# Opening of a fused four-layer kernel: loads on two queues, semaphores per use, second x slice early, first query rows copied from two queues

## The reference, cut to what matters

```python
x = x + attn(layernorm(x), Wq, Wk, Wv, Wo, Wg1, Wg2, norm_w)     # 16 batches x 256 x 128
x = x + moe(layernorm(x), router, w1, w3, w2, ws1, ws3, ws2)
x = x + conv_scan(layernorm(x), w_in, conv_w, conv_b, w_B, w_C, w_out)
x = x + fp4_ffn(layernorm(x), w_gate, w_up, w_down)
```

```python
q = silu(xn @ Wq);  k_raw = xn @ Wk;  v = xn @ Wv
z = cumlogsumexp([0, k_raw]);  k = exp(k_raw - z[1:]);  g = z[:-1] - z[1:]
q, k = rope(q), rope(k)                       # each twice as wide, cos and sin
o = causal_linear_attention(q, k, v, decay=g)
o = o * sigmoid(xn @ Wg1 @ Wg2)
x = x + (o * rsqrt(mean(o*o) + 1e-6) * norm_w) @ Wo
```

## Time and profile before

| | us |
|---|---|
| median of 3 runs | 609.23 (608.47 to 613.55) |
| the profiled execution, its time | 605.77 |
| the profiled execution, its span | 604.0 |
| PE busy | 542.9 (90% of the span) |
| DVE busy | 447.0 (74%) |
| POOL busy | 339.1 (56%) |
| ACT busy | 316.2 (52%) |
| mean granted TensorE clock | 0.973 |

### The profile page before, as it was taken

How to read it: one execution, slowest core, us unless ns; L and a number is a source line. 1 busy time by engine, 2 the same in 40 slices (tenths; PEclk the granted TensorE clock), 3 DMA queues, 4 the chain that set the end, 5 groups by cost and what they waited for, 6 DMA issues and landing times. The chain is left out here.

```text
span 604.0 us, 15157 instructions
## 1 busy us (share of the span) xinstructions
PE 542.9 (90%) x4517; PEld 444.8 (74%) x4518; DVE 447.0 (74%) x1179; ACT 316.2 (52%) x899; POOL 339.1 (56%) x514
## 2 busy tenths in 40 slices
PE   1799999999999898988999997998999999999966
PEld 1567667766777577788998986787788777887754
DVE  2689999899888549943457543478999999998873
ACT  2355766666666554415565652345545564556432
POOL 5468777777776622247567105556666775763231
PEclk9999999999999999998999998998999999999975
DMA  7000100110010155012522211100111111110000
GB/s 210 24 20 29 46 28 27 43 35 26 35 43 27 56 167 139 1 27 61 146 69 56 40 36 30 18 10 9 24 31 18 17 22 30 17 17 9 10 19 17
DMA packets 35193, 25.55 MB, mean 42 GB/s; under 512 B 4752, under 2 KB 31568, under 8 KB 35152
## 3 DMA queue, kind: packets, MB, share of 16 engines
q1 hardware_dynamic: 29264, 20.32, 11.5%
q0 software_dynamic: 5888, 4.72, 5.1%
HBM read 14.09 MB, written 6.75 MB: 34 GB/s over the span
## 5 line engine op out<-in xcount | busy, mean ns | idle before, releaser
L1149 PE MATMUL a_ps_a<-a_qx,a_kt 32*128 32x512 f32 x512 | 69.1, 628 | 1.0 <-DMA a_qx<-a_qs 1.0
L1712 POOL DMA_INDIRECT x<-yg_dram,pos x32 | 55.9, 1747 | 11.6 <-issue 11.6
L1316 POOL TENSOR_TENSOR d_hq<-d_fh_v,d_fh_scale 128x352 f32<-128x352 f32 x32 | 27.9, 888 | 61.3 <-DVE d_fh_v L1342 61.3
L442 POOL TENSOR_SCALAR_AFFINE_SELECT a_at<-a_at 128x512 f32<-128x512 f32 x80 | 50.5, 650 | 14.6 <-ACT a_at L523 14.6
L199 POOL DMA_INDIRECT rows<-xn_dram,slot_token x40 | 40.1, 1003 | 25.3 <-ACT c_rows L1478 11.0
L523 ACT ACTIVATE a_at<-a_ps_a 128x512 f32<-128x512 f32 x80 | 44.5, 600 | 11.6 <-PE a_ps_a L1149 10.0
L1521 DVE TENSOR_TENSOR c_hid<-c_act,c_ps 128x352 f32<-128x352 f32 x39 | 20.2, 518 | 36.4 <-ACT c_act L1464 36.4
L1149 PEld LDWEIGHTS a_ps_a<-a_qx,a_kt 32*128 32x128 f32 x512 | 31.7, 188 | 16.9 <-issue 16.3
L207 PE MATMUL d_ps_A<-d_xnT,wmix 128*128 128x256 f32 x128 | 37.1, 290 | 0.6 <-ACT d_silu L1794 0.6
L715 DVE TENSOR_TENSOR a_at<-a_ps_a,mask 128x512 f32<-128x512 f32 x48 | 32.8, 684 | 6.4 <-PE a_ps_a L1149 5.2
L208 PE MATMUL d_ps_A<-d_xnT,wmix 128*128 128x256 f32 x128 | 36.1, 282 | 0.0
(11 more groups left out here) (347 smaller groups left out, 1758.3 us busy)
## 6 DMA issues: line engine op xcount, KB each, us to landing
a_qx<-a_qs SPq DMA_DIRECT2D x64, 64.0 KB, 1.9
a_at<-in_L_ffn_w_eDF_dram SPq DMA_DIRECT2D x16, 176.0 KB, 3.2
yg_dram<-c_y SPq DMA_DIRECT2D x19, 128.0 KB, 1.8
xn_dram<-a_xn2s SPq DMA_DIRECT2D x16, 128.0 KB, 1.9
out_dram<-x SPq DMA_DIRECT2D x16, 128.0 KB, 1.9
w<-in_L_ffn_w_eFD_dram SPq DMA_DIRECT2D x2, 512.0 KB, 5.7
x<-in_L_attn_x_dram SPq DMA_DIRECT2D x1, 768.0 KB, 5.4
rows<-xn_dram,slot_token POOLq DMA_INDIRECT x40, 2.8
```

The source lines that it names most:

```text
L442: nc.gpsimd.affine_select(at[:, t, r, :, :], at[:, t, r, :, :], pattern=[[0, 4], [1, P]], compare_op=ALU.is_ge, fill=0.0, base=0, channel_ ...
L1149: last = nc.tensor.matmul(ps_a[:, r, :, :], kt[rows, b.par, c_, tile(t)], qx[rows, b.par, :, c_, tile(t)], start=(c_ == 0), stop=(c_ == 1))
L1712: nc.gpsimd.indirect_dma_start(out=x[:, t, :], out_offset=None, in_=g["yg_dram"][:, :], in_offset=bass.IndirectOffsetOnAxis(ap=g["pos"][:, ...
```

## The change

The loads are dealt out anew. ACT's queue takes the mask, Wg1 and Wg2, counted on a semaphore of their own, `s_wg`, for which alone PE's first transpose waits. SP's queue keeps x's first four tiles, Wk, Wq and Wv (`s_wq`, now three transfers); behind them come tiles 4 to 7 of x (`s_x2nd`, batches 2 and 3), the rope tables, the block mask, then Wo, norm_w and the router, which now count on `s_ws` with the two shared-expert weights. The rest of x comes in pieces of 12 tiles.

DVE begins with batch 0's statistics, behind the wait for x alone. `weights()` follows, in the same iteration: it rearranges Wk and Wq and makes the halves of 384 columns, then waits for ACT's product of Wg1 and Wg2 and makes those of the last 128. `weights_late()` scales Wo an iteration later, after batch 0's low half, behind a wait for the five transfers of `s_ws`. POOL zeroes `a_qx` after batch 0's `norm_sums` and no longer at the start. Of the first batch's four query transfers, SP issues two and ACT two, which ACT does after the steps of iteration -2, behind a wait for the scaled queries. PE waits for `s_prep_dve` at counts 5 and 6 before the gate product and the product with Wo of batch 0.

```diff
@@ SP
-            sp.dma_start(wg1[:, :], io["L0_attn_Wg1"]).then_inc(s_wq, 16)
-            sp.dma_start(wg2[:, :], io["L0_attn_Wg2"]).then_inc(s_wq, 16)
-            sp.dma_start(mask[:, :, :], io["c_mask"].rearrange("p (a b) -> p a b", a=3)).then_inc(g["s_const"], 16)
+            sp.dma_start(x[:, 4:8, :], xr[:, 4:8, :]).then_inc(s_x2nd, 16)
             sp.dma_start(rope[:, :, :], io["c_rope"].rearrange("p (a b) -> p a b", a=2)).then_inc(g["s_const"], 16)
             sp.dma_start(block[:, :], io["c_block"]).then_inc(g["s_const"], 16)
-            sp.dma_start(wo[:, :], io["L0_attn_Wo"]).then_inc(s_wq, 16)
-            sp.dma_start(normw[:, :], io["L0_attn_norm_w"].rearrange("(p a) -> p a", a=1)).then_inc(s_wq, 16)
-            sp.dma_start(router[:, :], io["L0_ffn_router_DE"]).then_inc(s_wq, 16)
+            sp.dma_start(wo[:, :], io["L0_attn_Wo"]).then_inc(s_ws, 16)
+            sp.dma_start(normw[:, :], io["L0_attn_norm_w"].rearrange("(p a) -> p a", a=1)).then_inc(s_ws, 16)
+            sp.dma_start(router[:, :], io["L0_ffn_router_DE"]).then_inc(s_ws, 16)
...
-            for a, b_ in ((4, 16), (16, 32)):
+            for a, b_ in ((8, 20), (20, 32)):
                 sp.dma_start(x[:, a:b_, :], xr[:, a:b_, :]).then_inc(g["s_x1"], 16)
...
-                    for h in range(4):
+                    for h in range(2 if j.m is None and j.off == 0 else 4):
@@ POOL
-            nc.gpsimd.memset(qx[:, :, :, :, :], 0.0).then_inc(s_zero, 1)
...
-                    pool.wait_ge(g["s_const"], 48)
+                    pool.wait_ge(g["s_const"], 32)
...
                 norm_sums(j + 3, mv[:, :, :], rstd[:, :], shift[:, :], s_ln1, s_xn, s_nb1)
+                if j.m is None and j.off == -3:
+                    nc.gpsimd.memset(qx[:, :, :, :, :], 0.0).then_inc(s_zero, 1)
@@ ACT
+            act.dma_start(mask[:, :, :], io["c_mask"].rearrange("p (a b) -> p a b", a=3)).then_inc(s_wg, 16)
+            act.dma_start(wg1[:, :], io["L0_attn_Wg1"]).then_inc(s_wg, 16)
+            act.dma_start(wg2[:, :], io["L0_attn_Wg2"]).then_inc(s_wg, 16)
             act.wait_ge(s_prep, 1)
...
+                if j.m is None and j.off == -2:
+                    act.wait_ge(s_zero, 2)
+                    act.wait_ge(s_qs, 1)
+                    for h in range(2, 4):
+                        act.dma_start(qx[h::4, 0, h, :, :].rearrange("p c n -> p (c n)"),
+                                      qs[h::4, 0, :, :].rearrange("p c n -> p (c n)")).then_inc(s_qx[0], 16)
@@ DVE
-            dve.wait_ge(s_wq, 16 * 8)
-            for n in range(2):
-                nc.vector.tensor_copy(wall[:, P * n:P * n + P].rearrange("p (r i s) -> p r s i", r=4, s=4),
-                                      wload[:, n, :].rearrange("p (r s i) -> p r s i", r=4, s=4))
-            nc.vector.tensor_scalar(wo[:, :], wo[:, :], normw[:, 0:1], 0.25, ALU.mult, ALU.mult).then_inc(s_prep_dve, 1)
...
+            def halves_of(cols, ready):
+                dve.wait_ge(s_prep_dve, ready)
+                nc.vector.tensor_copy(wallp[:, 0, cols], wall[:, cols]).then_inc(s_prep_dve, 1)
+                dve.wait_ge(s_prep_dve, ready + 1)
+                nc.vector.tensor_tensor(wallp[:, 1, cols], wall[:, cols], wallp[:, 0, cols].bitcast(F32),
+                                        ALU.subtract).then_inc(s_prep_dve, 1)
+            def weights():
+                dve.wait_ge(s_wq, 16 * 3)
...
+                halves_of(slice(0, 3 * P), 1)
+                dve.wait_ge(s_wx, 2)
+                halves_of(slice(3 * P, 4 * P), 3)
+            def weights_late():
+                dve.wait_ge(s_ws, 16 * 5)
+                nc.vector.tensor_scalar(wo[:, :], wo[:, :], normw[:, 0:1], 0.25, ALU.mult, ALU.mult).then_inc(s_prep_dve, 1)
...
-                if j.m is None and j.off + 2 in (0, 2):
-                    dve.wait_ge(*((g["s_x"], 16) if j.off + 2 == 0 else (g["s_x1"], 32)))
+                if j.m is None and j.off + 2 in (0, 2, 4):
+                    dve.wait_ge(*((g["s_x"], 16), (s_x2nd, 16), (g["s_x1"], 32))[(j.off + 2) // 2])
                 norm_stats(j + 2, stats, s_st1)
+                if j.m is None and j.off == -2:
+                    norm_aggr(j + 2, stats, mv, s_st1, s_nb1, s_ln1)
+                    weights()
...
-                norm_aggr(j + 2, stats, mv, s_st1, s_nb1, s_ln1)
-                if j.off == -2:
-                    dve.wait_ge(s_wx, 2)
...
+                if j.m is not None or j.off != -2:
+                    norm_aggr(j + 2, stats, mv, s_st1, s_nb1, s_ln1)
                 lower(j + 1)
+                if j.m is None and j.off == -1:
+                    weights_late()
@@ PE
-            pe.wait_ge(s_wq, 16 * 8)
-            pe.wait_ge(g["s_const"], 48)
+            pe.wait_ge(s_wg, 16 * 3)
```

More of the change, by code:

```diff
@@ L313, in phase_ab @@
         ps_s = ps_t[:, 0:2 * SLOTS]
-        s_wq, s_wx, s_zero = sem("s_wq"), sem("s_wx"), sem("s_zero")
+        s_wq, s_wg, s_x2nd, s_wx, s_zero = sem("s_wq"), sem("s_wg"), sem("s_x2nd"), sem("s_wx"), sem("s_zero")
         s_prep, s_prep_dve = sem("s_prep"), sem("s_prep_dve")
@@ L332, in phase_ab @@
         s_tab, s_w13, s_wh, s_wl = (sem(n) for n in ("s_tab", "s_w13", "s_wh", "s_wl"))
-        s_row, s_rowp, s_rowT = (sem(n) for n in ("s_row", "s_rowp", "s_rowT"))
+        s_row, s_rowp = sem("s_row"), sem("s_rowp")
         s_high, s_low, s_u, s_act, s_h, s_y, s_add = (sem(n) for n in ("s_high", "s_low", "s_u", "s_act", "s_h", "s_y", "s_add"))
@@ L699, in _ @@
             act.wait_ge(s_rowp, 1)
-            nc.scalar.activation(g["xT_first"][:, 0, :, :], halved(ps_m[:, 0:2 * P]), ACT.Copy).then_inc(s_rowT, 1)
+            nc.scalar.activation(g["xT_first"][:, 0, :, :], halved(ps_m[:, 0:2 * P]), ACT.Copy).then_inc(s_row, 1)
         @blk_.vector
         def _(dve):
-            dve.wait_ge(s_wq, 16 * 8)
-            for n in range(2):
-                nc.vector.tensor_copy(wall[:, P * n:P * n + P].rearrange("p (r i s) -> p r s i", r=4, s=4),
-                                      wload[:, n, :].rearrange("p (r s i) -> p r s i", r=4, s=4))
-            nc.vector.tensor_scalar(wo[:, :], wo[:, :], normw[:, 0:1], 0.25, ALU.mult, ALU.mult).then_inc(s_prep_dve, 1)
             def masked(b, t, r):
@@ L741, in state_decayed @@
                 if b.off == 0:
-                    dve.wait_ge(g["s_const"], 48)
+                    dve.wait_ge(g["s_const"], 32)
                 nc.vector.scalar_tensor_tensor(out=sx[:, b.par, :, :], in0=halved(ps_m[:, 0:N]), scalar=de[:, b.par, 1:2],
@@ L830, in lower @@
                                         ALU.subtract).then_inc(s_xnL, 1)
+            def halves_of(cols, ready):
[6 more added lines that the diff above has]
+                dve.wait_ge(s_wq, 16 * 3)
+                for n in range(2):
+                    last = nc.vector.tensor_copy(wall[:, P * n:P * n + P].rearrange("p (r i s) -> p r s i", r=4, s=4),
+                                                 wload[:, n, :].rearrange("p (r s i) -> p r s i", r=4, s=4))
+                last.then_inc(s_prep_dve, 1)
+                halves_of(slice(0, 3 * P), 1)
[4 more added lines that the diff above has]
+                nc.vector.tensor_scalar(wo[:, :], wo[:, :], normw[:, 0:1], 0.25, ALU.mult, ALU.mult).then_inc(s_prep_dve, 1)
             def body(j):
@@ L1018, in _ @@
             hidden(5, 2)
-            dve.wait_ge(s_rowT, 1)
+            dve.wait_ge(s_row, 2)
             nc.vector.tensor_tensor(g["xT_first"][:, 1, :, :], halved(ps_m[:, 0:2 * P]),
@@ L1157, in project_gate @@
                 done(pe, s_xn2t, b, ago=3)
+                if b.off == 0:
+                    pe.wait_ge(s_prep_dve, 5)
                 split_product(nc, ps_t[:, 0:N], lambda part: wallp[:, part, 3 * P:],
@@ L1164, in finish @@
                 done(pe, s_sq, b)
+                if b.off == 0:
+                    pe.wait_ge(s_prep_dve, 6)
                 if live(b + 2):
@@ L1207, in up @@
                     pe.wait_ge(s_copied, 5 * B)
-                    pe.wait_ge(s_prep_dve, 5)
+                    pe.wait_ge(s_prep_dve, 8)
                 if f == 0:
```

9 lines of the change are left out of this document (2 added, 7 removed).

## The result

| | before | changed |
|---|---|---|
| median of 14 runs each, taken in turns | 610.25 us (608.47 to 614.22) | 607.25 us (604.5 to 608.14) |
| ratio, changed to before | | 0.9925, 95% interval 0.9909 to 0.9942 |
| profiled execution, span | 604.0 us | 605.9 us |

The ratio is 4.6 us of 610.25 (3.5 to 5.6). The forecast was 6.3 us, so the change does less than I said. It is within 1%. The 607.25 lies inside the range, but close to its upper end of 607.5. Of the 4.4 us by which it missed 602.9, 1.0 us is the median of before, which was 609.23 when I forecast and 610.25 here.

What follows compares the result with a forecast made beforehand. The prediction took the opening's wait for transfers, then the query-row wait, as the bound, with PE's pace afterwards. 4.2 - 0.2 + 0.98 + 1.3 = 6.3 us gave 602.9 us, range 600.0 to 607.5.

Steps and rivals of the forecast that it cites:

- part 4: TensorE's pace: with the gap before the first score products gone, the clock rises earlier; 1.3 us won.
- Part 1: Opening: DVE's first statistics wait for x alone, at 4.4 instead of 8.56; 4.2 us won (3.7 to 4.7).
- Part 2: POOL's batch 0 `norm_sums` falls beside DVE's weight copies and halves; 0.2 us lost.
- the second: Rival: the clearing of `a_qx` starts first and holds DVE's last cast; 2.6 us lost, 605.5 us; chance 0.18.
- Both keep up, with 0.8 us or more to spare: Opening: DVE's weight work and PE's and ACT's way to ACT's copy finish before batch 0 needs them.
- Part 3: Query rows: SP and ACT issue two transfers each, so PE's wait before the score products goes; 0.98 us won.
- the third rival: Issues of the two queues do not overlap; only 1.6 to 2 us won, 607.4 us; chance 0.12.
- the first rival: No earlier rise of TensorE's pace; the first three terms hold, 5.0 us, 604.2 us; chance 0.22.
- After 27 us: Later batches follow at PE's pace, so whatever is won before 27 us moves the end by as much.

Runs made afterwards that it cites:

- held profile: The changed kernel's own profiled execution, span 605.9 us against 604.0 before; the clearing began 0.08 us ahead of the last cast, which took 3.50 us.
- second set: Follow-up runs on another chip, kernel before 611.2 us; the changed kernel again, unchanged: 607.9 us, ratio 0.9943.
- third set: Follow-up runs on yet another chip, kernel before 604.39 us; the changed kernel again, unchanged: 599.89 us, ratio 0.993.
- the kernel whose clearing waits: The changed kernel, with POOL's clearing of a_qx waiting for DVE's cast of the last 128 columns: 598.57 us, ratio 0.9915.
- the first set: One chip, before 604.78 us; changed kernel with clearing waiting (0.9915), ACT writing the cast half (0.9894), clearing in halves (0.9926), SP issuing all four query transfers (0.9915).
- the query rows alone: The kernel before, with only batch 0's query transfers split between SP and ACT: 611.47 us, one execution, where before took 609.66 to 614.38.
- the products of `ones`: Changed kernel, a_qx cleared by parity, identity loaded first, plus unread PE products: 606.98 us, 0.9912; ten for four behind batch 0's key transposes: 596.69 us, 0.9886.

## Why the prediction was right, and what it had wrong

The place, the sign and the class were right: faster, within 1%. The size was 6.3 us against 4.6 (3.5 to 5.6), and 4.1 over three comparisons. That the class came out right is partly luck, since 6.3 us is itself 1.0% and the mechanism of part 4 was wrong. By its own steps:

| term | forecast | held profile | second set | third set |
|---|---|---|---|---|
| PE's first product (parts 1 and 2) | 4.0 | 1.71 | 4.06 | 3.95 |
| wait for the query rows | 0.98 | 0.66 | 0.98 | 0.74 |
| the rest to batch 2's transposes: pace | 1.3 | 2.19 | 0.20 | 2.10 |
| batch 2's transposes | 6.3 | 4.56 | 5.24 | 6.79 |

Each entry is the earlier trace rows or the mark of before less the changed kernel's; "held profile" is the one of the first section. Before is one profile, measured beside none of these.

**Part 1, right.** 4.31 us for the forecast 4.2, by the mechanism given: x at 256 KB shares the engines with the mask. Where the cast was free, the chain behind kept its length, 4.45 to 10.35 in the third set, 5.90 us for 5.74.

**Part 2, right.** `norm_sums` took 2.25 us from 5.26 to 7.51, against 2.02 before: 0.23 lost for the forecast 0.2. L427, beside DVE's copies, took 0.95 against 0.71 before, L429 0.33 against 0.58, and L432 0.46 against 0.22. (The rival that this part points at is the second, not the first.)

**"Both keep up, with 0.8 us or more to spare": wrong in some executions.** Where the cast was free it held: DVE stood 1.10 and 1.17 us idle before the low half, in the third and the second set. Where the cast was held, DVE came 2.4 us late. Wv landed at 6.0, not 5.0 (at 5.7 in the two profiles with a free cast), as I had priced the mask's share for x but hardly for the three weights behind it. That took the margin of the cast over the clearing, which I had at 0.6 us, down to between +0.29 and -0.09 us: the clearing began near 7.4 as forecast, and the cast, which I had at 6.8, at 7.15 to 7.53 (7.80 where x was late). The rival gave the price, 2.6 us, and 2.4 were measured. I gave it 0.18 as a case of every execution; it is a case of some executions (one profile in three). That sentence is the step that failed on the way to PE's first product. In the median it costs less than its size: the kernel whose clearing waits has 0.9915, the changed kernel 0.9925, 0.9943 and 0.993 in other sets, a difference of 0.6 to 1.7 us that the intervals do not separate.

The Trainium skill (SBUF — State Buffer, "Who interferes with whom") says that a VectorE copy or cast in a two-port mode and GpSimd block each other, and that the one issued first wins. The runs here agree: a cast behind a clearing took 3.50 or 1.79 us, a cast ahead of it 0.23 or 0.25.

**Part 3, right.** The issues overlap (four in 1.44 us), which refutes the third rival, whose rule in the Trainium skill (Perfetto Trace Analysis, "DMA Instruction — HWDGE (DVE, Sync)") is not borne out between these two queues. With the part undone, PE waited 0.92 us again. In two of three profiles of the changed kernel 0.24 and 0.32 remain, since there PE was already at full pace and reached the products sooner.

**Part 4, wrong in its reason.** Before, the rise came near 31.6. It came at 23.5, 25.4 and 21.5 in three profiles of the changed kernel, at 25.7, 26.2, 23.2 and 26.4 in the first set, in the order above, and at 35.0 with the query rows alone. (Within the score products it is read from their starts, which come in fours, 0.85 us apart at the lower pace and 0.43 at the full one. The expectation above that has 22.7 and 24 had misread two of them.) From PE's last long idle time (2.3 us) to the rise, with no more than 0.64 us of idle time in between, that is 3.5 us in the first and 12.9 in the last. There is no count of work that these rows follow. I had built the term on one profile of before, where the rise was one draw as well. Without it the sum is 5.0, the first rival (604.2), and less some executions in which the cast is held, by a third of 2.4, it is 4.2, beside 4.1 measured. This last step is worked out afterwards and not shown: it takes the share from three profiles, and leaves out the pace, which the table has at 0.20 to 2.19, 1.5 in the mean. With the pace in it, the marks at batch 2 give 5.5 us in the mean, and less the 0.3 outside the span 5.2: about 1.1 us more than the medians show, and no run accounts for that. One profile of before, with a pace of its own, may be the reason.

**After 27 us, right for this change.** The gain of 4.56 at batch 2 is 4.53 at 269 us, and in the third set 6.79 is 6.69 there and 6.58 at the clearing of `d_hs` (361.64). A larger gain was not carried along, as the products of `ones` show: 1.97 us more at batch 2 were 0.23 at 269 us.

Open: what sets the moment of the rise; the 1.1 us between the marks and the medians; what the 0.3 us outside the span are; why the third stage takes 102 us in one set, and what its "remote" releaser is.

## What to carry to other kernels

When an engine is freed early, list what the engine that can hold it, or be held by it, will start in that moment (here POOL beside DVE), and compare the two start times to a tenth of a microsecond: a long fill that costs nothing on its own engine can hold a 0.2 us cast for its whole length, in some executions only, so one profile shows it or hides it. See to it too that the edit of an experiment acts in the profile that it is read from: a wait that never waits proves nothing. Put such a fill where the other engine waits anyway, or split it. And price a second transfer beside the first for everything that is queued behind, not only for the one that you look at; a change of a few us is best read at marks that both kernels have, since the spans of two profiles can differ by more than that elsewhere.
